# SyncE issues the stores of x2 ahead of the load of a later batch's context

## What is computed

```python
x = _layernorm(x + attn(x))                       # x1 below
q = einsum('bsd,ed->bse', x, Wq) + bq
k = einsum('btd,ed->bte', context, Wk) + bk
v = einsum('btd,ed->bte', context, Wv) + bv
x = _layernorm(x + softmax(q k^T / 16) v)         # x2 below: the change is here
x = _layernorm(x + experts(x) + shared(x))        # the router reads x2 transposed
```

## Time and profile before

| what | us |
|---|---|
| median of 3 runs | 1034.51 |
| the three runs | 1034.51, 1027.21, 1036.3 |
| the profiled execution, its own time | 1028.26 |
| the span in its trace | 1026.3 |
| stretch of the steps 2 to 17 in it, roughly | 436 to 672 |
| busy in the span: PE, DVE, ACT, POOL | 845.0, 638.6, 474.5, 401.9 |

### The profile page before, as it was taken

How to read it: one execution, slowest core, us unless ns; L and a number is a source line. 1 busy time by engine, 2 the same in 40 slices (tenths; PEclk the granted TensorE clock), 3 DMA queues, 4 the chain that set the end, 5 groups by cost and what they waited for, 6 DMA issues and landing times. The chain is left out here.

```text
span 1026.3 us, 19460 instructions
## 1 busy us (share of the span) xinstructions
PE 845.0 (82%) x6042; PEld 679.9 (66%) x6043; DVE 638.6 (62%) x1479; ACT 474.5 (46%) x1098; POOL 401.9 (39%) x421
## 2 busy tenths in 40 slices
PE   3578888888888686788887779879996999999993
PEld 2455555555555344677776668658886999988883
DVE  5367777767777630355555644676654777757776
ACT  1125665666566671254454434324542555533443
POOL 4333333433343000565566554107772000037773
PEclk8569999999999986899899997989998999999998
DMA  2888999999999716345544542135754555534543
GB/s 72 212 200 183 225 246 254 227 231 240 253 222 220 200 43 129 54 94 124 114 107 89 124 103 104 62 108 194 262 185 144 170 169 164 164 110 138 176 127 98
DMA packets 194421, 162.67 MB, mean 159 GB/s; under 512 B 82480, under 2 KB 179376, under 8 KB 191280
## 3 DMA queue, kind: packets, MB, share of 16 engines
q1 hardware_dynamic: 177712, 134.50, 51.7%
q0 software_dynamic: 6144, 16.79, 5.0%
q10 hardware_dynamic: 10496, 10.49, 3.3%
HBM read 81.91 MB, written 75.37 MB: 153 GB/s over the span
## 5 line engine op out<-in xcount | busy, mean ns | idle before, releaser
L598 DVE TENSOR_REDUCE neg_m<-ps_s 128x2 f32<-128x512 f32 x256 | 169.1, 688 | 38.1 <-PE ps_s L352 37.5
L488 ACT ACTIVATE probs<-ps_t 128x512 f32<-128x512 f32 x256 | 147.1, 598 | 76.6 <-PE ps_t L358 72.2
L352 PE MATMUL ps_s<-k_stack,q_stack 48*128 48x256 f32 x512 | 119.1, 333 | 53.5 <-DVE neg_m L598 42.5
L352 PEld LDWEIGHTS ps_s<-k_stack,q_stack 48*128 48x128 f32 x512 | 76.2, 194 | 110.1 <-DVE neg_m L598 56.1
L111 PE MATMUL ps_f<-w_cross,w_sgu 128*128 128x512 f32 x552 | 133.5, 391 | 0.6 <-issue 0.6
L2045 POOL DMA_INDIRECT w_gu<-expert_outputs,pos x64 | 64.8, 1012 | 154.2 <-DMA expert_outputs<-low 135.6
L358 PE MATMUL ps_t<-q_stack,k_stack 49*128 49x256 f32 x512 | 118.3, 331 | 2.7 <-ACT probs L488 2.7
L111 PEld LDWEIGHTS ps_f<-w_cross,w_sgu 128*128 128x128 f32 x552 | 100.8, 188 | 19.9 <-issue 0.7
L111 PE MATMUL ps_g<-w_qkv,x_hl 128*128 128x512 f32 (+1 forms) x384 | 91.0, 387 | 18.5 <-DVE w_qkv L524 11.4
L111 PEld LDWEIGHTS ps_g<-w_qkv,x_hl 128*128 128x128 f32 x384 | 66.0, 214 | 36.3 <-DVE w_qkv L524 11.1
L1619 PEld LDWEIGHTS ps_f<-w_sdn,hid_hl 128*128 128x128 f32 x576 | 74.7, 191 | 13.1 <-DVE hid_hl L1903 5.2
(11 more groups left out here) (208 smaller groups left out, 1716.1 us busy)
## 6 DMA issues: line engine op xcount, KB each, us to landing
stacks<-q_hl SPq DMA_DIRECT2D x48, 256.0 KB, 2.8
stacks<-k_hl SPq DMA_DIRECT2D x48, 256.0 KB, 3.5
q_stack<-stacks SPq DMA_DIRECT2D x32, 384.0 KB, 6.2
k_stack<-stacks SPq DMA_DIRECT2D x32, 384.0 KB, 9.5
expert_rows<-no_rows ACTq DMA_DIRECT2D x16, 640.0 KB, 5.3
low<-expert_rows SPq DMA_DIRECT2D x79, 128.0 KB, 2.1
expert_outputs<-low SPq DMA_DIRECT2D x79, 128.0 KB, 1.8
heads_out<-o_sb SPq DMA_DIRECT2D x32, 256.0 KB, 9.8
```

The lines of the kernel that those rows point to most:

```text
L352: by_query = pe.matmul(ps_s[n % 2][:, k * N:(k + 1) * N], q[q_rows, slab, k * P:(k + 1) * P], kk[q_rows, slab, :], start=True, stop=True)
L488: act.activation(probs[:, n % RING], ps_t[n % 2].rearrange("p (t q) -> p t q", t=TT), ACT.Exp).then_inc(exp_done, 1)
L598: dve.tensor_reduce(neg_m[c][:, :, row], ps_s[n % 2].rearrange("p (t k) -> p t k", t=TT), AX.X, ALU.max, negate=True).then_inc(max_done, 1)
```

## The change

The load of the context is taken out of `load` into a function of its own, and in a step it is called last, behind the stores of x2. In the opening step (-1) it follows `load` directly, as before. No DMA, no wait and no byte is added or removed, and no other engine's list is touched.

```diff
                 sp.dma_start(xr[b.par][:], one(x_dram, b, "o p t d -> p (o t) d")).then_inc(xr_in[b.par], 16)
+
+            def load_context(b):
                 if b.least(2):
                     sp.wait_ge(c_lo, b.n - 1)
                 sp.dma_start(cT[b.par][:], cT_dram[:, :, bass.ds(b.n * N, N)]).then_inc(cT_in[b.par], 16)
@@
                 if i.static and i.n == -1:
                     load(i + 1)
+                    load_context(i + 1)
                     for n, name in enumerate(RAW):
@@
                     for part in range(2):
                         sp.dma_start(x2T_hl[part].rearrange("(c p) t -> p c t", p=P)[:, :, bass.ds(r.n * N, N)],
                                      x2_hl[:, part].bitcast(F32)).then_inc(x2T_out, 16)
+                if (i + 2).inside():
+                    load_context(i + 2)
```

## The result

The changed kernel takes 1001.84 us, the median of 4 runs (994.84 to 1014.04), against 1035.4 us before (4 runs, 1027.21 to 1037.87). The ratio is 0.967, with a 95% interval of 0.958 to 0.975: faster by 2.5 to 4.2%. The forecast was 1004, with a range from 995 to 1016.

The account below looks back on a forecast made before the run. Each step was held by VectorE's wait for the x2 store, late behind SyncE's wait on `c_lo`. 27.9 + 4.3 + 2.4 - 6.8 = 27.8 us less gave 1000.5 for the profiled execution, median 1004, range 995 to 1016.

Parts of the forecast that it names:

- The wait and its cause: VectorE's L1195 waits for the x2 store, held in SyncE's list by `c_lo`: each step about 2.5 us longer.
- What a step takes without it: Loop step, XQ to XQ on TensorE, without the store's wait: 12.0 us, read from steps 2 and 6.
- The first term: Loop steps 2 to 13: 11 steps fall from 14.53 to 12.0 us each, 27.9 us less.
- SyncE's way to the store: SyncE is free at t + 3.5, issues the x2 store at t + 5.1; moved load and heads cost nothing.
- The exit of the loop: Step 13 to 14, on leaving the loop: from 16.35 to 12.0 us, 4.3 us less.
- Step 14: Its scores and values on TensorE return to 2.4 GHz without the idle time: 2.4 us less.
- the sum's last term: PV2 at the low clock in 4 of 12 steps, 1.7 us each: 6.8 us lost.
- rival B: PV2 at the low clock in every step, 13.69 us a step: 14.3 us less, 1017 us; chance 0.12.
- C: Rival: no low clock at all, nor in steps 14 and 15: 37.3 us less, 994 us; chance 0.12.
- A: The forecast itself: TensorE's chain bounds the step at 12.0 us, some low-clock PV2; 996 to 1013 us; chance 0.70.
- D: Rival: x2 store stays late behind the heads' transfers, L1195 still waits; up to 1031 us; chance 0.04.
- E: Rival: TensorE at 1.2 GHz in scores, values and PV2 of every step, 15.8 us each: 1046 us; chance 0.02.

Follow-up runs that it names:

- two-buffer kernel: Kernel before, SyncE's list untouched, with x2 in two buffers by batch parity, each with its own semaphore: 998.5 us, ratio 0.966.
- softmax-first kernel: Changed kernel with ScalarE's cast of the transposed x2 moved from ahead of the two exponentials to behind them: 993.5 us, ratio 0.967 to the kernel before.
- wait kept: Changed kernel with SyncE's wait on `c_lo` kept ahead of the x2 store too, the load staying behind the stores: 1017.2 us, ratio 0.986.
- changed again: The changed kernel run once more, unchanged, for its spread and a second trace: 997.2 us, ratio 0.967 to the kernel before.
- the load 4.5 us ahead: Changed kernel with the context's load ahead of the x2 store again, but for the next step's batch: 1000.1 us, ratio 0.970 to the kernel before.

## Why the prediction was right, point by point

**The wait and its cause.** Right. L1195 waited for a store that SyncE held behind the wait on `c_lo`; the two-buffer kernel shows that L1195's wait for the store was the whole price, and the kernel with the wait on `c_lo` kept shows that this wait alone costs 1.45 us a step.

**What a step takes without it.** Right: 12.0 us, read from step 2, against 11.92 measured. The chain through TensorE bounds it: the softmax-first kernel takes a wait of TensorE out of it, and the step falls to 11.70. The first term, 27.9 us, measured 28.8.

**SyncE's way to the store.** Right in each part: SyncE was through 1.6 us before x2 was ready (1.5 forecast), the store left at t + 5.2 (5.1), the context's load 0.16 us behind GpSimd. The heads went out 0.04 us behind L1200 in the step shown and 0.39 ahead of it in the next, where 0.2 ahead was forecast, and VectorE's L1126 waited for nothing. The store's landing turned out shorter, 2.3 us in the median instead of the 2.8 of the earlier trace rows.

**The exit of the loop.** 4.7 us, forecast 4.3: nothing else held VectorE there. Step 14 gave 3.9 us where the sum had 2.4. Its scores and values were back at the full clock (2.4 forecast), and its PV2 was too; that part stood in the sum's last term only. Both terms were read from one execution of before, and against the second one they are 3.8 and 1.1 us.

**The low clock.** Here the sum was off. It took 4 low PV2 in 12 steps, 6.8 us lost; in the profiled execution there was none in them, and none in the two other traces of the changed kernel either. The count was wrong, not the price: step 15, with its low PV2, took 13.53 us in the profiled execution and 11.90 in the second trace, 1.6 more, where the sum had 1.7. The estimate stood on four steps of before, and these lie among steps with idle time ahead of their scores. Across all traces the kernels in which L1195 waits for the store (before twice, wait kept) have 10 low PV2 of 45; the seven traces without that wait have 2 of 105, both in step 15. That the idling causes them is a reading that these counts allow, but no run here varied it alone, and it is not enough by itself: in the kernel with the wait kept, the steps 3 to 10 idle 1.06 to 1.45 us ahead of their scores and none of their PV2 is low; the three low ones are in the steps 11 to 13. The Trainium skill's rule on short idles between groups of matmuls (page "TensorE: Matmul & The Clock Gate", section "A second HAM failure mode: psum-queue depth-cycling"), which would have given rival B, was not borne out: the chain still idles at its transposes in each step (0.35 and 0.67 us in step 14), and the clock of the stretch was 0.99 to 1.00.

**The rivals.** In the profiled execution it went as C: 28.8 + 4.7 + 3.9 = 37.4 us, as C had it (37.3), though step 15 kept its low PV2; the second trace of before would have given 31.3. The median came out near A's all the same, since I had put it above the profiled time, and of the four runs the profiled one was the fastest. Where one slower execution was traced (1001.02 us), its extra time lay in the stages ahead (445.7 against 438.8 us). So the forecast is closer than its parts, and that is luck: the sum for the profiled execution was 5.7 us too high (1000.5 against 994.84), mostly by the low clock, and the margin from it to the median was 3.5 us too small (3.5 against 7.0). B, D and E did not show.

## What to carry to other kernels

A wait in the list of an engine that only issues DMAs delays everything behind it, so order that list by when each item's wait is over and by who needs its result first, not by subject. A step of the same loop that happens to be free of the stall, here step 2, gave the time without it to 0.1 us. Where, as here, whole executions differ by 10 us for reasons outside the changed stage, cut the stage out of each trace and compare that.

## What I had not expected of the hardware

- A store issued right behind a load of as many bytes on the same queue landed later. Issue to landing was 2.8 us in the median with the load 0.6 us ahead of it (before, and the two-buffer kernel, where nobody waits for the store), and 2.3 where no load stood close ahead (changed, changed again, wait kept, and the load 4.5 us ahead). With the load between the stores it was 2.6; there the load of x goes out later, closer ahead of the store. That it is the other transfer's traffic was not tried by itself. The changed kernel's second trace, last row of the answer on L839:

```profile
DMA to landing us min/median/max: 2.3/2.3/2.3
```

- One program's stages ahead of step 2 took from 435.5 to 452.2 us in ten traces, with mean clocks from 0.91 down to 0.86 in them; these 16.7 us are half of the 33.6 that the change took off the span.
